# Two fused decoder layers on one core: inside each slot of attention, the weighing of the values moves ahead of the row maxima of a later head group

## The reference

```python
x = _layernorm(x + _L0_attn_ref(x, ...))        # self attention, 256 keys
x = _layernorm(x + _L0_xattn_ref(x, ctx, ...))  # cross attention, 1601 keys
x = _layernorm(x + _L0_ffn_ref(x, ...))         # mixture of experts
x = _layernorm(x + _L1_attn_ref(x, ...))        # state space scan
x = _layernorm(x + _L1_xattn_ref(x, ctx, ...))  # cross attention, 1601 keys
x = _layernorm(x + _L1_ffn_ref(x, ...))         # quantised feed forward

# one cross attention
q = (x @ w_q + b_q).reshape(B, Lq, 16, 8)
k = (context @ w_k + b_k).reshape(B, -1, 16, 8)
v = (context @ w_v + b_v).reshape(B, -1, 16, 8)
scores = jnp.einsum('bqhd,bkhd->bhqk', q, k) * scale
weights = jax.nn.softmax(scores, axis=-1)
out = jnp.einsum('bhqk,bkhd->bqhd', weights, v).reshape(B, Lq, D) @ w_o + b_o
```

## Time and profile before

| | |
|---|---|
| median of 3 runs | 3814.59 us (3813.77 to 3818.99) |
| profiled execution, its own time | 3814.54 us |
| its span in the trace | 3812.7 us |
| TensorE busy | 3414.2 us, 90% |
| VectorE busy | 2877.0 us, 75% |
| ScalarE busy | 2315.7 us, 61% |
| GpSimd busy | 1093.5 us, 29% |
| self attention | up to about 330 us of the span |
| first cross attention | about 336 to 1735 us |
| second cross attention | about 2300 to 3735 us |

### The profile page before, as it was taken

One profiled execution on the slowest core, in us unless ns is written; L12 is line 12 of the kernel. 1 busy time (PEld: TensorE's weight loads), 2 busy tenths in 40 slices (PEclk: granted clock), 3 DMA queues, 4 the chain that ended last, 5 costly groups with the idle time before them and its releaser, 6 DMA issues. The chain is left out here.

```text
span 3812.7 us, 97480 instructions
## 1 busy us (share of the span) xinstructions
PE 3414.2 (90%) x38912; PEld 1681.8 (44%) x38912; DVE 2877.0 (75%) x3923; ACT 2315.7 (61%) x4557; POOL 1093.5 (29%) x1895
## 2 busy tenths in 40 slices
PE   6885999999999999994999582999999999999998
PEld 3442444444444444433666481444444444444445
DVE  5776788888888888864443796888888888888874
ACT  3663676777777677772332540677777777767773
POOL 5552223222222232201666002222322222233202
PEclk9997999999999999996999796999999999999999
DMA  4332222222222222200000002222223222222210
GB/s 101 76 81 56 62 56 60 54 66 68 64 55 63 55 59 59 69 22 26 1 0 1 0 0 58 54 64 55 60 57 77 60 58 63 55 60 54 66 30 24
DMA packets 160675, 194.99 MB, mean 51 GB/s; under 512 B 31172, under 2 KB 118632, under 8 KB 160248
## 3 DMA queue, kind: packets, MB, share of 16 engines
q1 hardware_dynamic: 160072, 188.49, 21.1%
q10 hardware_dynamic: 176, 0.61, 0.0%
HBM read 27.95 MB, written 2.10 MB: 8 GB/s over the span
## 5 line engine op out<-in xcount | busy, mean ns | idle before, releaser
L600 ACT ACTIVATE cross_Pr<-cross_sT 128x512 f32<-128x512 f32 (+1 forms) x3584 | 1834.4, 563 | 766.8 <-PE cross_sT L520 765.8
L663 DVE TENSOR_REDUCE cross_nm<-cross_ring 128x2 f32<-128x802 f32 x2048 | 1974.7, 991 | 321.7 <-PE cross_ring L486 293.3
L520 PE MATMUL cross_sT<-cross_Q,cross_K 64*128 64x256 bf16 x13312 | 1043.8, 273 | 48.6 <-ACT cross_Pr L600 42.6
L539 PE MATMUL cross_oT<-cross_Pr,cross_V 128*9 128x256 f32 x13312 | 1029.9, 381 | 0.0
L520 PEld LDWEIGHTS cross_sT<-cross_Q,cross_K 64*128 64x128 bf16 x13312 | 510.9, 95 | 771.3 <-ACT cross_Pr L600 637.9
L486 PE MATMUL cross_ring<-cross_K,cross_Q 64*128 64x401 bf16 x4096 | 661.7, 336 | 63.2 <-DMA cross_K<-cross_kparts 34.6
L407 POOL TENSOR_TENSOR cross_mp<-cross_nm,cross_one 128x8 bf16<-128x8 f32 x128 | 25.9, 203 | 1371.6 <-DVE cross_nm L668 1371.6
L539 PEld LDWEIGHTS cross_oT<-cross_Pr,cross_V 128*9 128x9 f32 x13312 | 197.7, 88 | 412.7 <-issue 246.0
L486 PEld LDWEIGHTS cross_ring<-cross_K,cross_Q 64*128 64x128 bf16 x4096 | 198.9, 94 | 203.3 <-DVE cross_nm L663 106.7
L1102 DVE TENSOR_TENSOR moe_rc<-moe_r,moe_bank 128x512 f32<-128x512 f32 x128 | 87.9, 687 | 170.5 <-ACT moe_r L993 170.5
L874 POOL TENSOR_TENSOR moe_hh<-moe_r,moe_rc 128x512 f32<-128x512 f32 x128 | 162.6, 1270 | 153.4 <-DVE moe_rc L1102 152.7
(11 more groups left out here) (286 smaller groups left out, 3003.3 us busy)
## 6 DMA issues: line engine op xcount, KB each, us to landing
cross_K<-cross_kparts SPq DMA_DIRECT2D x1152, 100.1 KB, 2.3
cross_in<-in_ctx_T_dram SPq DMA_DIRECT2D x32, 600.4 KB, 5.7
self_QK<-self_parts SPq DMA_DIRECT2D x144, 128.0 KB, 2.8
cross_Q<-cross_qparts SPq DMA_DIRECT2D x288, 64.0 KB, 2.1
self_in<-in_x_T_dram SPq DMA_DIRECT2D x16, 128.0 KB, 2.3
cross_Q<-cross_mst SPq DMA_DIRECT2D x128, 16.0 KB, 1.8
out_dram<-X SPq DMA_DIRECT2D x8, 256.0 KB, 2.3
self_QK<-self_mst SPq DMA_DIRECT2D x64, 16.0 KB, 1.8
```

The costliest lines, as they stand in the source:

```text
L520: mm = pe.matmul(sT[0:r, cfg.sT_bank(b, u + j), (c % 2) * S:(c % 2 + 1) * S], K[ROWS * j:ROWS * (j + 1), pair, t, s:s + r], Q[ROWS * j:ROW ...
L539: mm = pe.matmul(oT[32 * j:32 * j + VR, 0:S], V[0:r, b % VB, c, 4 * g + j, :], Pr[0:r, slot, (c % 2) * S:(c % 2 + 1) * S], start=(c == 0), ...
L600: act.activation(Pr[0:r, u % NPR, 0:nc_ * S], sT[0:r, cfg.sT_bank(b, u), 0:nc_ * S], ACT.Exp).then_inc(exped, 1)
L663: dve.tensor_reduce(nm4[:, g % 2, t, :, pk, blk], R.rearrange("p (j n) -> p j n", j=2)[:, :, 0:cfg.block], AX.X, ALU.max, negate=True).the ...
```

## The change

The order within a slot becomes B, PV, A, MT. Nothing else is altered: the same instructions with the same waits, in the same slots. Only TensorE's order changes.

```diff
@@ -104,7 +104,7 @@
         out += [(ont, ("ONT", 0)), (bias, ("BIAS",)), (fin, ("OUT", 0)), (ln, ("LN",))]
-        rank = {op: n for n, op in enumerate(("B", "A", "PV", "MT"))}
+        rank = {op: n for n, op in enumerate(("B", "PV", "A", "MT"))}
         return sorted(out, key=lambda e: (e[0], rank.get(e[1][0], 9)))
...
```

## The result

| | before | after |
|---|---|---|
| median of 4 runs each | 3816.79 us | 3981.59 us (3976.33 to 3983.13) |
| ratio | | 1.043, 95% interval 1.0412 to 1.0448 |
| profiled execution's span | 3812.7 us | 3979.8 us |

The forecast was 3962 us, 148 above the execution profiled before; the trace grew by 3979.8 - 3812.7 = 167.1. Nearly all of it, 165.8, lies in the three attentions. From the first to the last B of each, the self attention takes 330.4 us after 277.4 (+53.0), the first cross attention 1391.8 after 1334.6 (+57.1), the second 1390.1 after 1334.3 (+55.7). The stretch between the two cross attentions, with the experts and the scan, took 673 us before and after.

What follows compares the result with a forecast made beforehand. TensorE's program with a few waits bounds a turn, ScalarE's loop the plain slots. Cross attentions 102 us plus self attention 46 make 148 over 3814.54, so 3962 us; range 3880 to 4020.

Steps and rivals of the forecast that it cites:

- The bound and the plain slots: Cross attentions: ScalarE's loop keeps plain slots at 1.30 us; TensorE's new order needs 1.26, so no change.
- rival 2: Plain slots of the cross attentions lose too, 1.38 against 1.30 us: 89 us on top, 4051 us; chance 0.10.
- The longer waits on reads: Cross turn: MT after a double A waits 0.64 us, before 0.2; K in slot 9 waits, +0.57.
- The changes of shape: Cross turn: one more per fp32 unit, 0.10 us each, 0.7 a turn; two more for MT, +0.20 in slot 10.
- The count of 15.5 turns: Turns counted in each attention: 31 × 3.3 = 102 us for both cross attentions, 46 us for the self attention.
- The rule on tiling modes: Trainium skill: changing tiling mode drains TensorE, moving among tiles of a mode doesn't; trace showed 0.09 to 0.11 us.
- rival 1: Only the changes of shape cost, cross and self attentions: 71 us in sum, 3886 us; chance 0.10.
- The self attention: A turn there gets 3.0 us longer as units wait for later reads; 15.5 turns, 46 us.
- Rival 3: Faster, as PV covers A's waits in the cross attentions: 3779 us, 3708 if shapes were free; chance 0.06.
- Rival 4: No change, as ScalarE's loop hides all, as in plain slots: 3815 us; chance 0.04.
- ScalarE's wait for B: In the changed kernel's trace, ScalarE's total wait for B goes up by about 148 us.

Runs made afterwards that it cites:

- half reads: VectorE's reduction of an A unit over half the columns: old order 3700.39 us, new order 3803.41 us, ratios to the old kernel 0.9699 and 0.9967.
- the three slots: Old kernel with PV ahead of A only in slots 23, 37 and 51 of a cross turn: 3875.95 us, ratio 1.0164.
- reads of an eighth: VectorE's reduction of an A unit over an eighth of the columns: old order 3678.03 us, new order 3753.95 us, ratios to the old kernel 0.9637 and 0.9839.

## Why the prediction was right, point by point

*The bound and the plain slots.* As written: 1.30 before and after, B to PV 0.53 to 0.55 and A to B 0.17 to 0.20, the two distances that no row had shown. The 0.20 of a plain slot holds a wait for ScalarE: behind the double A of slot 37, which is longer than the loop, A to B is 0.17 (1025.03 + 0.18 to 1025.38). So TensorE's own work in a plain slot is about 0.54 + 0.55 + 0.17 to 0.18, that is 1.26 to 1.27, and rival 2 did not come, by a cover of about 0.03.

*The longer waits on reads.* Shown by half reads (the loss falls from 165 to 103 us) and by the three slots (0.64 each, as written). Slot by slot, new less old: slots 1 to 3 +0.47 (0.45 written), slot 9 +0.60 (0.57), 23 to 25 +0.44 and 37 to 39 +0.45 (0.41), 51 to 53 +0.66 (0.61).

*The changes of shape.* 0.11 for an fp32 unit (slots 1, 4, 5, 7, 32, 48), 0.24 for MT in slot 10; written down were 0.10 and 0.20. In slots 13 and 55 the price was 0.20, not 0.10. K and V there also wait for the read of the A of the slot before, 12 or 54. Those slots are short, about 1.07, and their A now comes late, and these waits I left out. With reads of an eighth the two slots lose 0.08 each, so the wait is 0.12. Slots 12 and 13 of a turn of the changed kernel, from the view of all engines:

```profile
1165.66 0.34 PE L486 MATMUL cross_ring<-cross_K,cross_Q 64*128 64x401 bf16 x2
...
1166.05 2.04 DVE L663 TENSOR_REDUCE cross_nm<-cross_ring 128x2 f32<-128x802 f32 x2 [0.48 <-PE cross_ring L486]
...
1166.71 0.34 PE L486 MATMUL cross_ring<-cross_K,cross_Q 64*128 64x401 bf16 x2
1167.10 0.30 PEld L463 LDWEIGHTS cross_ring<-cross_in,cross_wk 97*128 97x128 f32 x2 [0.30 <-DVE cross_nm L663]
```

The A of slot 12 starts at 1165.66, its read ends at 1166.05 + 0.99 = 1167.04, and K starts 0.06 after that; the A of slot 13 is still unread.

With 0.02 in slot 11 and some hundredths elsewhere this makes 3.8 in a turn, not 3.3. The count of 15.5 turns was a little high: 57.1 us from the first B to the last are 15 turns of 3.8. Together, 113 us for 102.

*The rule on tiling modes.* With the reads of an eighth one more change of shape costs 0.08 to 0.11, two cost 0.21 to 0.22. The Trainium skill ("TensorEngine Tiling (Array Packing)", Key Properties) says that a change of tiling mode drains TensorE, and these figures agree with it. The changes of shape explain at most 76 of the 113 us in the cross attentions (what is left there with reads of an eighth, which still holds a wait of slot 9), and not the rest. So they are about two thirds of the loss there, and the longer waits a third or a little more; rival 1, which had the shapes alone, fell.

*The self attention.* 53.0 us, 46 written. The turn's 3.15 for 3.0 is close, and so are its parts: slots 1 and 2 +0.74 (0.73 written), 3 and 4 +0.98 (0.93), slot 5 +1.09 (1.07), slots 7 and 0 +0.34 (0.26). About 11 us come from the clock (below), which no term of mine had. Without them the stage would have lost 42: the first turn lost only 1.24, the last three 2.32, 2.28 and 0.01, and some turns of the old order were 0.2 to 0.6 above 18.12. So 15.5 turns of the full price were too many, and that 46 lies near 53 is in part luck.

*Rivals 3 and 4.* Rival 3, the gain, is true of five slots and 27 us, where A waits and no ring unit follows in the slot. The waits of A's weight loads as a whole didn't go: they rose from 106.7 to 277.5, though much of that now lies under PV; of A's matmuls themselves they rose from 22.6 to 63.1. A part of the rise is in slots 16, 30 and 44, which have two A and no PV: their second A now waits for the read of the late A of the slot before, and they take 1.41 to 1.42 for 1.30. That takes back what slots 17, 31 and 45 gain. Rival 4, no change, fell with the result. The view of the changed kernel's waits, which answers to the earlier trace rows, with the copy of MT by ScalarE:

```profile
PEld cross_ring L486 <- DVE cross_nm L663: 277.5, 535, 1.5
...
ACT cross_mst L586 <- PE cross_ring L502: 141.5, 96, 43.4
```

*One sign misjudged.* I expected ScalarE's wait for B to rise by the whole loss. It rose by 43.8 us in the cross attentions (765.8 to 809.6) and 30.8 in the self attention (84.5 to 115.3). Another 71.7 stand ahead of ScalarE's copy of MT, 86.8 to 141.5 and 25.3 to 42.3: it reaches MT in its own program before the next B, so the lateness is booked there. The 21 that are left of the 167 I did not trace.

## What to carry to other kernels

In a ring of two buffers that a slow reader empties, where the writer places its fill within a period has a price of its own: fill early and put the work that needs no buffer between one fill and the next. Here the same swap lost where another ring unit followed soon, gained where the fill itself had to wait and none followed, and did nothing in plain slots, so it is to be decided slot by slot from the distances in a timeline; three slots of 56 made 61 us worse, five others 27 us better. When an order is changed, count the changes of matmul shape on the way, each about 0.1 us here, and every slot whose unit waits for a buffer filled in the same slot or in a short one just before.

## What the hardware showed that I had not expected

TensorE's granted clock fell within the self attention. It was 1.00 in the turns of before, and 0.96 over the changed kernel's self attention; six turns, at 0.86 to 0.92, took 22.4 to 24.4 us in place of 21.27, 11 us in all. The drops lie in slots 3 and 5 of a turn. In such a place B and PV took this long:

```profile
205.46 0.81 PE L520 MATMUL self_sT<-self_QK 64*128 64x256 bf16 x8
206.20 1.89 PE L539 MATMUL self_oT<-self_Pr,self_V 128*9 128x256 f32 x16
208.03 0.61 PE L493 MATMUL self_ring<-self_QK 64*128 64x256 bf16 x4
```

PV to A is 1.83 for 0.98: the 1.2 GHz level in place of 2.4. TensorE was busy 16.08 of 21.27 us in a turn at full clock, with idle stretches of 0.57 to 1.11 us among its matmuls, against 14.99 of 18.12 us in a turn of before. Ahead of each drop stood two or three such stretches, of 0.57 to 0.96 us. It was back at full speed before the turn ended. With half reads and the new order the self attention ran at 1.00 throughout, with turns of 17.96, and the run with the new order in the self attention alone fell to 0.96 again. With reads of an eighth and the old order, two turns ran at 0.91, each behind a single idle stretch of 2.1 to 2.3 us. So the drops stand where idle time was added; that it caused them was not tried by itself.
